# Attention and mixture-of-experts kernel on one core: halves of the attention output made by GpSimd and turned by a DMA, maxima of two heads by one instruction, and a new plan of the slots

## What is computed

```python
qkv = x @ Wqkv.T + bqkv                          # 16 heads of 16 features
attn = softmax(q @ k.T / 4)
coh = sigmoid(tanh(concat(x, cond) @ Wc1.T + bc1) @ Wc2.T + bc2)
mod = attn * coh; mod = mod / (mod.sum(-1) + 1e-8)
mod = (1 - fi) * mod + fi * fa                   # fa: one softmax over positions per batch
x = x + (mod @ v) @ Wout.T + bout

gate = rms_norm(x) @ wg_W + wg_b + cond @ gg_W + gg_b
cw = softmax(gate), kept for its two largest of 8 experts
h1 = relu(x @ W1[e] + b1[e]); h2 = relu(h1 @ W2[e] + b2[e])
x = x + sum over the two experts e of cw[e] * (h2 @ W3[e] + b3[e])
```

## Time and profile before

| what | us |
|---|---|
| runs | 939.65, 936.78, 946.73; median 939.65 |
| the profiled execution | 950.3, of which 948.4 is the span |
| from the first B tile to the last batch's first | 56.3 to 463.2 |
| a steady batch of 16 slots | 57.3 (231.4 to 288.7, 288.7 to 346.0) |
| last batch and start of the experts | 463.2 to about 530 |
| experts | to 948.4 |

### The profile page before, as it was taken

The page is one execution under the profiler, slowest core; times in us unless marked ns, Lnnn a source line. Parts: engine busy times, 40 slices in busy tenths (PEclk is TensorE's granted clock), DMA queues, the critical chain, the costliest instruction groups (busy, mean ns, idle before and its releaser), DMA issues.

```text
span 948.4 us, 23132 instructions
## 1 busy us (share of the span) xinstructions
PE 878.1 (93%) x6806; PEld 514.9 (54%) x6807; DVE 699.8 (74%) x1680; ACT 581.5 (61%) x1256; POOL 406.3 (43%) x446
## 2 busy tenths in 40 slices
PE   5799999999999999998888989799999999999994
PEld 2232333333333333332231678678888888888873
DVE  6768889888998988989996387768865555555442
ACT  3147877877778878787586657655444444444441
POOL 4313435555646656553253326643553233223322
PEclk9679999999999999999896899989999999999998
DMA  6543243443526426171053187875644333333432
GB/s 207 121 80 71 66 53 91 97 113 79 97 82 109 122 60 127 42 124 48 13 173 114 26 243 179 192 191 100 129 74 57 46 57 52 51 46 55 66 49 25
DMA packets 109434, 88.36 MB, mean 93 GB/s; under 512 B 63816, under 2 KB 102216, under 8 KB 107024
## 3 DMA queue, kind: packets, MB, share of 16 engines
q1 hardware_dynamic: 95664, 68.05, 31.6%
q0 software_dynamic: 13296, 18.23, 11.6%
q10 hardware_dynamic: 384, 0.93, 0.3%
HBM read 44.97 MB, written 33.31 MB: 83 GB/s over the span
## 4 chain that ended last, share of the span: by engine, by line
PE 74%; DVE 11%; ACT 5%; DMA 4%; issue 3%; POOL 1%; SPq 1%; DVEq 0%; ACTq 0%; POOLq 0%
PE bank L1053 30%; PE bank L950 10%; PE bank L898 10%; PE bank L1069 9%; PE bank L885 8%; DVE mx L1320 5%; PE bank L874 4%; ACT arena L1203 2%; PE bank L956 2%; DVE arena L1627 1%; DMA w_b<-mxp 1%; PE bank L1008 1%; DMA out<-y,y_dest 1%; POOL arena L654 1%; ACT arena L1151 1%
## 5 line engine op out<-in xcount | busy, mean ns | idle before, releaser
L1320 DVE TENSOR_REDUCE mx<-bank 128x1 f32<-128x512 f32 x512 | 324.3, 682 | 49.2 <-PE bank L874 46.1
L1203 ACT ACTIVATE arena<-bank 128x512 f32<-128x512 f32 x512 | 277.4, 596 | 70.4 <-PE bank L885 68.5
L1239 ACT ACTIVATE hf<-bank,small 128x256 f32<-128x256 f32 (+1 forms) x312 | 133.5, 456 | 190.2 <-PE bank L1053 188.3
L753 POOL DMA_INDIRECT out<-y,y_dest x71 | 130.5, 1838 | 239.5 <-DVE y_dest L1608 207.8
L1053 PE MATMUL bank<-hh,arena 128*128 128x256 f16 (+1 forms) x1248 | 198.6, 265 | 0.1
L874 PE MATMUL bank<-arena 48*128 48x512 f16 x512 | 170.8, 396 | 16.8 <-DVE mx L1320 12.8
L1589 DVE TENSOR_TENSOR hl<-hf,hh 128x256 f16<-128x256 f32 (+1 forms) x304 | 112.6, 395 | 93.7 <-ACT hh L1243 93.2
L885 PE MATMUL bank<-arena 49*128 49x512 f16 x512 | 164.5, 394 | 14.6 <-DMA arena<-w_b 6.3
L1053 PE MATMUL bank<-hl,arena 128*128 128x256 f16 (+1 forms) x624 | 163.6, 263 | 0.0
L898 PE MATMUL bank<-arena 128*17 128x512 f32 x1024 | 139.6, 618 | 0.9 <-ACT arena L1203 0.9
L885 PEld LDWEIGHTS bank<-arena 49*128 49x128 f16 x512 | 39.1, 94 | 177.5 <-ACT arena L1203 149.2
(11 more groups left out here) (228 smaller groups left out, 971.3 us busy)
## 6 DMA issues: line engine op xcount, KB each, us to landing
raw<-in_we SPq DMA_DIRECT2D x16, 1024.0 KB, 5.2
arena<-parts_dram SPq DMA_DIRECT2D x84, 128.0 KB
parts_dram<-arena SPq DMA_DIRECT2D x64, 128.0 KB, 1.8
arena<-in_xT SPq DMA_DIRECT2D x8, 512.0 KB, 4.5
arena<-in_x SPq DMA_DIRECT2D x8, 512.0 KB, 5.9
...
```

The lines of the kernel that those rows point to most:

```text
L753: pool.indirect_dma_start(out=out, out_offset=bass.IndirectOffsetOnAxis(ap=y_dest[:, par, s:s + 1], axis=0), in_=y[:, par, s, :], in_offse ...
L1203: nc.scalar.activation(pr[:, s % TT, n, :], b_bank[no % B_RING][:, :], ACT.Exp, scale=SCALE).then_inc(b_read, 1)
L1239: nc.scalar.activation(hf[which][:, m, 0:n], layer[which][m // 2][:, m % 2 * TS:m % 2 * TS + n], ACT.Relu, bias=bias[which][:, bass.ds(e, ...
L1320: V.tensor_reduce(mx[:, g % 2, c, s % TT:s % TT + 1], a_bank[no % A_RING][:, :], X, ALU.max).then_inc(a_read, 1)
```

## The change

- **Maxima of two heads by one instruction.** The three A banks are one tensor. A0 and A1 of a slot stand in neighbouring banks and are reduced together, 128 x 1024 to two columns (`reduce_pair`); A2 and A3 are reduced singly. `a_read` counts three per slot. A0 and A1 wait for R2 of the slot before, A2 for R3 of the slot before, and A3 for the pair of its own slot.
- **Attention output.** POOL writes both halves into `att_parts` (`split_output`), and SP turns 128 x 1024 fp16 of them into `attT` by one DMA transpose (`turn_output`): no `at` task, no eviction by ACT and DVE. `op` waits for both transposes. In the last batch ACT and DVE make the second column half's parts.
- **Expert rows.** POOL makes both halves (`send_rows`, slots 7 and 11); in the last batch ACT and DVE do, as before.
- **Plan.** `coh` is one task of eight matmuls in slot 2, `op` stands in slots 5 to 8, `c1` 0 in slot 11, `count` in slot 13, slots 3 and 4 have none. `vs` is evicted by ACT. Routing is five steps in slots 10 to 14: the first key comes from `logit < 0` after the maximum was taken off, with the expert's number in eighths. The squares move to slots 6 to 9.
- The scaling of the maxima is a scalar_tensor_tensor with a tensor of ones.

```diff
+A_BANKS = ((1, 0, 2, 0), (2, 1, 0, 2))
+PAIR_BANKS = (slice(0, 2), slice(1, 3))
+A_READS = 3
...
 PLAN = {
-    0: [("coh", 0, 0), ("v", 0, 1)],
-    1: [("coh", 1, 0), ("ot", 3, -1)],
-    2: [("at", 1, -1), ("coh", 2, 0)],
-    3: [("coh", 3, 0), ("op", 0, -1)],
-    4: [("op", 1, -1)],
-    5: [("ot", 0, 0), ("op", 2, -1)],
-    6: [("op", 3, -1)],
-    7: [("vs", 0, 0), ("c1", 0, 1)],
-    8: [("pj", 0, 2)],
+    0: [("v", 0, 1)],
+    1: [("ot", 3, -1)],
+    2: [("coh", 0, 0)],
+    3: [],
+    4: [],
+    5: [("ot", 0, 0), ("op", 0, -1)],
+    6: [("op", 1, -1)],
+    7: [("vs", 0, 0), ("op", 2, -1)],
+    8: [("op", 3, -1), ("pj", 0, 2)],
     9: [("ot", 1, 0), ("v", 3, 1)],
     10: [("pj", 2, 2)],
-    11: [("at", 0, 0), ("v", 1, 1)],
-    12: [("pj", 1, 2), ("count", 0, -1)],
-    13: [("ot", 2, 0), ("pj", 3, 2)],
+    11: [("c1", 0, 1), ("v", 1, 1)],
+    12: [("pj", 1, 2)],
+    13: [("ot", 2, 0), ("count", 0, -1), ("pj", 3, 2)],
     14: [("v", 2, 1)],
     15: [("c1", 1, 1)],
 }
-ROUTE_AT = {(9, 0): 0, (10, 1): 1, (11, 0): 2, (11, 1): 3, (12, 0): 4, (13, 1): 5}
+ROUTE_AT = {(10, 1): 0, (12, 0): 1, (12, 1): 2, (13, 0): 3, (14, 1): 4}
...
@@ sync
+        def turn_output(i, b):
+            sp.wait_ge(att_low[i], b + 1)
+            if b > 0:
+                evicted(sp, ("op", 3, b - 1))
+            sp.dma_start(attT[:, i, :, :, :].rearrange("p t c n -> p (t c) n"),
+                         att_parts[i][:, :, :, :].rearrange("p t c e -> p (t c e)"), transpose=True).then_inc(att_turned[i], 16)
...
+            if at == 13 and 0 <= b < B:
+                turn_output(0, b)
+            if at == 3 and 0 <= b - 1 < B:
+                turn_output(1, b - 1)
@@ gpsimd
+        def split_output(i, b):
+            c = slice(i * P, (i + 1) * P)
+            pool.wait_ge(faded, 2 * b + i + 1)
+            after(pool, att_turned[i], 16 * b)
+            nc.gpsimd.tensor_copy(att_parts[i][:, :, 0, :], att[:, :, c]).then_inc(att_high[i], 1)
+            pool.wait_ge(att_high[i], b + 1)
+            nc.gpsimd.tensor_tensor(att_parts[i][:, :, 1, :], att[:, :, c], att_parts[i][:, :, 0, :], ALU.subtract)\
+                .then_inc(att_low[i], 1)
@@ tensor, a_tile
-            if no >= A_RING:
-                pe.wait_ge(a_read, no - A_RING + 1)
+            if n == 3:
+                pe.wait_ge(a_read, A_READS * s + 1)
+            elif s > 0:
+                pe.wait_ge(a_read, A_READS * s - (0 if n == 2 else 1))
@@ vector
+        def reduce_pair(s):
+            g = s // TT
+            dve.wait_ge(a_ready, s * G + 2)
+            V.tensor_reduce(mx[:, g % 2, 0:3:2, s % TT], score_banks[:, PAIR_BANKS[s % 2], :], X, ALU.max).then_inc(a_read, 1)
...
-            V.tensor_scalar(mxp[:, g % 2, 0:G * TT], mx[:, g % 2, :, :].rearrange("p h t -> p (h t)"), -1.0 / SHIFT_UNIT, None, ALU.mult)\
-                .then_inc(mx_split, 1)
+            V.scalar_tensor_tensor(mxp[:, g % 2, 0:G * TT], mx[:, g % 2, :, :].rearrange("p h t -> p (h t)"),
+                                   -1.0 / SHIFT_UNIT, ones[:, 0:G * TT], ALU.mult, ALU.mult).then_inc(mx_split, 1)
```

202 lines of the change are left out of this document (108 added, 94 removed).

## The result

The changed kernel took 1007.91 us in the median of four runs (1000.2 to 1011.89), the kernel before, run beside it, 942.59. The ratio is 1.0688, with a 95% interval of 1.0596 to 1.078. I had forecast 953.3 us, +1.5%, and a range of 934 to 968. The direction was right, the size was under a quarter of what came, and the time lies far outside the range.

A forecast was written before the change was run, and what follows sets the result against it. PE's order of work bounds the steady attention batches (PE 55.7 of 57.3 us); +2.0 +1.6 -1.2 -0.6 +0.8 -0.4 = +2.2 a batch, +15.4 over seven, +13.8 in all: 964.1 profiled, scaled to 953.3 us (+1.5%), range 934 to 968.

The forecast's parts named there:

- The pair: A3 waits for the two-bank reduce of 1.21 us, starting 1.95 into the slot: +2.0 and +1.6 us per batch.
- Rival A: Faster: two banks are reduced in about 0.9 us or less, so A3 isn't delayed; 928 us, chance 0.15.
- I put the port at 0 in the sum: DVE instructions blocked by POOL instructions that read SBUF: counted as 0 in the sum and made a rival.
- Rival C: Slower: six routing instructions in slots 12 and 13 wait for POOL, 1.5 us a batch; 964 us, chance 0.15.
- Slot 13 loses about 0.8: Four chained routing instructions, some 0.75 us, stand behind slot 13's pair, and count must wait; about 0.8 us lost.
- -0.6 in all: DVE's and ACT's lighter load, with routing moved to slots 12 and 13: -0.6 us per steady batch.
- The empty slots: Slots 3 and 4, without tasks, last 2.6 and 3.0 us as the next B0 waits for ACT; +0.8 us per batch.
- `coh` as one task costs the same: The coherence product as one task in slot 2 costs the same eight fp32 matmul pairs, so no time was added.
- The transposes: Output transposes taken off PE: -1.2 us per batch; the DMA transposes land in about 4 us, hidden.
- Rival D: Slower: the shift's DMAs or op wait for the large transpose, 1 us a batch and more; 960 and up, chance 0.10.
- The last batch and the experts: Last batch -1 us, with pairs in ten slots but DVE lighter; experts -0.6 us, as one at goes.

The follow-up runs named there:

- e9: The changed kernel with only the scaling of the maxima moved from DVE to ACT: 989.08 us, ratio 1.0465.
- e12: The changed kernel with the scaling on ACT and the coherence product moved from slot 2 to slot 3: 977.69 us, ratio 1.0395.
- e13: The changed kernel, pair kept, with scaling on ACT, coherence product in slot 3, bias sum back in slot 2, count last in slot 13: 969.97 us.
- e11: The changed kernel without the pair, scaling on ACT, coherence product in slot 3, bias sum back, count last in slot 13: 947.36 us.
- e14: The 947.36 us version (no pair) with count in slot 14, routing step 3 behind slot 13's tasks, step 4 in slot 15, last-batch tables later: 942.47 us.

## Why the prediction was wrong

**The chain of versions.** Each step takes one cause out of the changed kernel; a batch goes from 67.47 us to 57.63, the kernel before has 57.57.

```
changed kernel                                    67.47
scaling off DVE (e9)                              64.09   -3.4
coherence product out of slot 2 (e12)             63.11   -1.0
bias sum back, count last in slot 13 (e13)        60.56   -2.6
pair undone (e11)                                 58.62   -1.9
count in 14, routing 3 behind slot 13 (e14)       57.63   -1.0
```

The size of a step depends on the order in which they are taken, above all because each also changes the clock; the sum doesn't. Each row is one trace.

**The pair: right.** A3 at 1.96 for 1.95, the reduce 1.225 us for 1.21, the batch +2.84 on the kernel before for +3.6. Rival A is out: two banks in one instruction save 0.14 us against two reduces of 0.684, and the A tile waits for the whole.

**"I put the port at 0 in the sum": the step that failed first.** The rows for it were there: the scaling takes 0.74 us in slot 6, and I had named the rule. I failed to follow the new POOL order past the scaling. The change lets the last bias sum and `fade` run back to back in slot 2, beside an instruction on which the pair, A3 and the slot's task depend. Rival C had the right mechanism in the wrong place and at a third of its price: it priced six routing instructions at 0.3 to 0.6. Measured are 1.53 us for one scaling in slot 2, about 1.0 in slot 6 in some batches, and 0.68 for one routing instruction. The Trainium skill (SBUF — State Buffer, Who interferes with whom) says that issue order, not the form of the operation, decides who blocks, and that ACT waits for nobody. The trace agrees on both: 1.70 to 1.73 us in either form on DVE, at most 0.218 on ACT, also where the sum of values had begun before it. The same section says that whoever starts first holds the port for its whole instruction; by that alone I would price a hold at one POOL instruction at most. The 1.70 us row is longer than either of the two beside it (0.75 and 1.27), so here a waiting DVE instruction was passed over by the next POOL instruction in line.

**"Slot 13 loses about 0.8": mis-sized.** The lateness of the routing was seen, and the wait of `count` behind it is 0.80 us, as said. What the sum left out is what stands behind `count`: a projection that needs the bank of `ot`, whose division DVE does only after the routing and the last maxima. That wait is 1.50 us. With the held instruction and the half clock that follows, slots 12 and 13 lost 2.8 us (11.52 for 8.72) where "-0.6 in all" stood. The run with `count` last removes 2.05 us of slot 13, the one with `count` in slot 14 another 1.8.

**The empty slots: right at full clock.** In batches whose clock stayed up, slots 3 and 4 took 2.60 and 3.07 us (forecast 2.6 and 3.0), as in one batch of the run with the bias sum moved and one of the run with the scaling on ACT. In the changed kernel they are 4.09 and 3.65, for the most part at half clock.

**"`coh` as one task costs the same": right in matmuls, wrong in consequence.** It takes 1.96 us at full clock. But in one piece in slot 3 it was followed by half clock in 10 of 24 batches, in two runs of eight in 2 of 18.

**The clock had no term at all.** The second to the seventh batch went from 7 to 85 us at half clock. Slots 3 to 5 lasted 12.4 us in the changed kernel, and 9.80 with the same order on PE in single batches of five other versions in which the clock stayed up, so about 2.6 us a batch are the clock there, and 0.8 more in slot 13's projection. Neither is an independent loss: each begins behind a long wait or the thin product. A forecast that adds new waits in PE's order should price them twice, once as the wait and once as what follows at half clock.

**The transposes: right, as far as seen.** They land in 3.1 us and PE doesn't wait. Rival D is out. The -1.2 us was not tried alone; that the undisturbed batches of the version of 942.5 us last 56.0 to 56.5, some 0.4 to 1.3 us below the steady ones before (56.9 to 57.3), fits it.

**The last batch and the experts:** -1.6 forecast, -0.5 measured, which the spread of that part between versions (482 to 496 us) doesn't tell from nothing.

What stays open: why the first batch is longer with the pair, by 10 us in the kernel before and 2 to 6 elsewhere; whether the run of thin matmuls or the empty slot beside it matters; and which of the smaller waits sets slots 4 and 5 in the last versions. The half clock in these comes and goes from batch to batch with the same order of work, so a term for it can only be a range.
